# Delta twice in memory, slots per engine for the preparation of a unit, and the gate one step earlier

## The reference, cut to what matters

```python
xz = einsum('blc,ec->ble', xs, in_w); xi, z = xz[..., :d_inner], xz[..., d_inner:]
xi = silu(conv4(xi) + conv_b)
dt, Bm, Cm = split(einsum('bld,ed->ble', xi, xp_w))          # 6, 16 and 16 columns
delta = softplus(einsum('blr,dr->bld', dt, dt_w) + dt_b)
dA = exp(delta[..., None] * A)
dBu = delta[..., None] * Bm[:, :, None, :] * xi[..., None]
def step(h, inp):
    dA_t, dBu_t, C_t = inp
    h = dA_t * h + dBu_t
    return (h, einsum('bds,bs->bd', h, C_t))
y = (ys + xi * Dp) * silu(z)
out = einsum('bld,cd->blc', y, out_w)
```

## Time and profile before

| | us |
|---|---|
| median of 3 executions (5672.62 to 5676.45) | 5675.06 |
| the profiled execution | 5685.29 |
| its span, first to last instruction | 5683.5 |
| DVE busy | 3950.0 (69%) |
| PE busy | 3607.9 (63%) |
| ACT busy | 2759.5 (49%) |
| POOL busy | 2643.2 (47%) |

### The profile page before, as it was taken

The page is one execution under the profiler, slowest core; times in us unless marked ns, Lnnn a source line. Parts: engine busy times, 40 slices in busy tenths (PEclk is TensorE's granted clock), DMA queues, the critical chain, the costliest instruction groups (busy, mean ns, idle before and its releaser), DMA issues.

```text
span 5683.5 us, 44812 instructions
## 1 busy us (share of the span) xinstructions
PE 3607.9 (63%) x11400; PEld 1333.7 (23%) x11400; DVE 3950.0 (69%) x3478; ACT 2759.5 (49%) x3178; POOL 2643.2 (47%) x1276
## 2 busy tenths in 40 slices
PE   6566675666756667566675666656667566675666
PEld 2211222112321123211232112321123211232112
DVE  6478675786757867578675776748766487665876
ACT  4454454444544445444454544554545545455444
POOL 2266432664336643366433664336643365433664
PEclk8677786777767778677776777767777777776777
DMA  1367303663036630466304663046630466304762
GB/s 30 85 162 175 90 12 91 163 167 90 12 97 162 162 91 11 104 157 163 90 10 109 157 164 86 8 109 161 159 87 7 109 168 159 83 4 111 172 160 68
DMA packets 186995, 597.66 MB, mean 105 GB/s; under 512 B 30956, under 2 KB 31704, under 8 KB 185912
## 3 DMA queue, kind: packets, MB, share of 16 engines
q1 hardware_dynamic: 186680, 594.18, 42.5%
HBM read 485.03 MB, written 46.14 MB: 93 GB/s over the span
## 4 chain that ended last, share of the span: by engine, by line
issue 31%; PE 23%; DVE 21%; POOL 11%; ACT 9%; DMA 4%; SPq 1%; DVEq 0%; POOLq 0%; ACTq 0%
DVE ps L1152 7%; POOL arena L1242 5%; DVE arena L1157 4%; PE ps L620 4%; PE ps L612 4%; DVE arena L1045 3%; DMA arena<-dl 3%; POOL arena L1225 3%; PE ps L516 3%; POOL arena L1231 2%; PE ps L464 2%; PE ps L562 2%; PE ps L507 2%; PE ps L640 1%; ACT arena L746 1%
## 5 line engine op out<-in xcount | busy, mean ns | idle before, releaser
L1242 POOL TENSOR_TENSOR arena<-arena 128x1024 f32<-128x1024 f32 x768 | 1799.8, 2350 | 1268.1 <-DVE arena L1157 872.7
L1157 DVE TENSOR_TENSOR_SCAN arena<-arena,ps 128x1024 f32<-128x1024 f32 x768 | 1756.3, 2287 | 151.2 <-POOL arena L1242 38.1
L640 PE MATMUL ps<-arena,spread 96*128 96x512 bf16 x1536 | 611.5, 499 | 1115.5 <-DVE arena L1157 964.2
L880 ACT ACTIVATE arena<-arena,a_all 128x1024 f32<-128x1024 f32 x768 | 872.8, 1143 | 782.1 <-DMA arena<-dl 624.8
L1152 DVE TENSOR_TENSOR ps<-ps,arena 128x1024 f32<-128x1024 f32 x768 | 929.9, 1211 | 420.9 <-PE ps L640 420.9
L658 PE MATMUL ps<-arena,gather 128*32 128x512 f32 x3072 | 725.6, 846 | 83.1 <-POOL arena L1242 83.1
L1186 POOL TENSOR_TENSOR x<-x,arena 96x512 f32<-96x512 f32 x128 | 209.4, 1636 | 848.7 <-DVE arena L963 848.7
L640 PEld LDWEIGHTS ps<-arena,spread 96*128 96x128 bf16 x1536 | 120.7, 109 | 1778.4 <-DVE arena L1157 1328.1
L612 PE MATMUL ps<-arena,w_in 96*96 96x512 f32 x512 | 367.3, 885 | 63.2 <-DMA arena<-xq 63.2
L620 PE MATMUL ps<-arena,w_in 96*96 96x512 f32 x256 | 223.6, 1022 | 252.6 <-ACT arena L843 252.6
L1134 DVE TENSOR_TENSOR arena<-ps,arena 96x1024 f32<-96x1024 f32 x64 | 78.1, 1220 | 370.2 <-ACT arena L864 370.2
(11 more groups left out here) (149 smaller groups left out, 5409.6 us busy)
## 6 DMA issues: line engine op xcount, KB each, us to landing
arena<-dl SPq DMA_DIRECT2D x768, 512.0 KB, 5.4
arena<-bc SPq DMA_DIRECT2D x128, 512.0 KB, 6.2
arena<-arena SPq DMA_DIRECT2D x576, 64.0 KB, 2.2
dl<-arena SPq DMA_DIRECT2D x64, 384.0 KB, 3.5
xq<-in_x SPq DMA_DIRECT2D x8, 1536.0 KB, 8.9
arena<-xq SPq DMA_DIRECT2D x64, 192.0 KB, 3.8
out<-x SPq DMA_DIRECT2D x64, 192.0 KB, 2.1
arena<-xq SPq DMA_DIRECT2D x64, 191.8 KB, 3.2
```

The lines of the kernel that those rows point to most:

```text
L640: mm = pe.matmul(ps[:, bank + c, :], spread[:, r, :], sp[:, i, b, c * 512:(c + 1) * 512], start=True, stop=True)
L880: act.activation(da[:, m % DAS, :], dbc[:, m % DBC, :], ACT.Exp, scale=a_all[:, v // 2, m:m + 1]).then_inc(da_ready, 1)
L1157: dve.tensor_tensor_scan(hs[:, m % 2, :], da[:, m % DAS, :], driven, 0.0, ALU.mult, ALU.add).then_inc(h_ready, 1)
L1242: pool.tensor_tensor(pr[:, m % PRS, :], hs[:, m % 2, :], cmat[:, v % 2, :], ALU.mult).then_inc(pr_ready, 1)
```

## The change

Three things are changed together.

1. Layout: the partition of a state is now d * 16 + s. Delta is stored twice (`COPIES = 2`), as rows (channel, copy), so that one broadcast reads 16 different rows and writes each to 8 partitions in a row. `bmat` and `cmat` now take 16 rows one after the other, 8 times. `delta_out` counts 32 per unit.
2. Slots: each engine has its own. PE's z goes from slot 1 to slot 2, DVE's Delta from 4 to 5, ACT's first two parts from 5 and 6 to 7 and 8. On SP the xs copy goes to slot 5, the store of B and C to 6, the load of `bmat` to 7, the stores of Delta to 8, the load of `cmat` to 10, the parts to 10, 11 and 11.
3. Gate: S_GATE is 1. The silu of xi waits for the first sum of the unit before last (`y_acc`) and only the silu of z waits for its gate (`yz_ready`).

```diff
-S_XI, S_SILU, S_DT, S_SOFT, S_U, S_R, S_P2 = 0, 1, 3, 4, 5, 6, 7
-S_GATE, S_SKIP, S_OUT = 2, 4, 8
+PE_XI, PE_Z, PE_DT = 0, 2, 3
+ACT_SILU, ACT_DT, ACT_SOFT, ACT_P0, ACT_P1 = 1, 3, 4, 7, 8
+DVE_DELTA = 5
+POOL_U, POOL_R, POOL_P2 = 5, 6, 7
+SP_SHIFT, SP_BC, SP_B, SP_DL, SP_C = 5, 6, 7, 8, 10
+SP_P0, SP_P1, SP_P2 = 10, 11, 11
+S_GATE, S_SKIP, S_OUT = 1, 4, 8
...
                     sync.dma_start(dbc[:, m % DBC, :],
-                                   a["dl"][v % 2][g * DG:(g + 1) * DG, :].rearrange("(o d) n -> o d n", o=1)
-                                   .broadcast_to([NS, DG, L])).then_inc(dbc_in[m % DBC], 16)
+                                   a["dl"][v % 2][g * DG:(g + 1) * DG].rearrange("d c (o n) -> (d c) o n", o=1)
+                                   .broadcast_to([DG * COPIES, NS // COPIES, L])).then_inc(dbc_in[m % DBC], 16)
...
+                    if slot == SP_DL:
+                        sync.wait_ge(delta_ready, V + 1)
+                        for c in range(COPIES):
+                            sync.dma_start(a["dl"][i][:, c, :], delta).then_inc(delta_out, 16)
...
-                    if slot == S_SILU:
+                    if slot == ACT_SILU:
                         act.preload_act_table(ACT.Silu)
                         if v >= 2:
-                            act.wait_ge(yz_ready, V - 1)
+                            act.wait_ge(y_acc, (V - 2) * GPB + 1)
                         for c in range(2):
                             act.wait_ge(xi_ps, 2 * V + c + 1)
                             act.activation(xi[:, i, c * 512:(c + 1) * 512], ps[0:DI, 6 + c, :], ACT.Silu,
                                            bias=small_all[:, q, KC:KC + 1]).then_inc(xi_ready, 1)
+                        if v >= 2:
+                            act.wait_ge(yz_ready, V - 1)
                         for c in range(2):
                             act.wait_ge(z_ps, 2 * V + c + 1)
...
-    state_row = np.arange(128) % DG
+    state_row = np.arange(128) // NS
```

More of the change, by code:

```diff
@@ L52 @@
 DBC = 3
+COPIES = 2
 DAS = 3
@@ L391, in prep @@
                     q, i = divmod(v, 2)
-                    if slot == S_DT + 1:
+                    if slot == SP_SHIFT and v + 1 < UNITS and v >= 1:
+                        shifted(v + 1)
+                    if slot == SP_BC:
                         sync.wait_ge(bc_evac, V + 1)
                         sync.dma_start(a["bc"][i], bc_rows).then_inc(bc_out, 16)
[L395 to L399, removed]
+                    if slot == SP_B:
                         sync.wait_ge(bc_out, (V + 1) * 16)
@@ L402, in prep @@
                         if v >= 2:
-                            sync.wait_ge(pr_ready, (V - 1) * G)
[L404 to L408, removed]
+                            sync.wait_ge(bu_ready, (V - 1) * G)
+                        sync.dma_start(bmat[:, i, :], a["bc"][i][0:NS, :].rearrange("(o s) n -> o s n", o=1)
+                                       .broadcast_to([DG, NS, L])).then_inc(b_in, 16)
+                    if slot == SP_DL:
+                        sync.wait_ge(delta_ready, V + 1)
+                        for c in range(COPIES):
+                            sync.dma_start(a["dl"][i][:, c, :], delta).then_inc(delta_out, 16)
+                    if slot == SP_C:
+                        if v >= 2:
+                            sync.wait_ge(pr_ready, (V - 1) * G)
+                        sync.dma_start(cmat[:, i, :], a["bc"][i][NS:2 * NS, :].rearrange("(o s) n -> o s n", o=1)
+                                       .broadcast_to([DG, NS, L])).then_inc(c_in, 16)
+                    for k, at, done in ((0, SP_P0, part0), (1, SP_P1, part1), (2, SP_P2, part2)):
                         if slot == at:
@@ L601, in prep @@
                     q, i = divmod(v, 2)
-                    if slot == S_XI:
+                    if slot == PE_XI:
                         pe.wait_ge(xs_in[i], (p * QUADS + q + 1) * XSL)
@@ L615, in prep @@
                             mm.then_inc(xi_ps, 1)
-                    if slot == S_SILU:
+                    if slot == PE_Z:
                         for c in range(2):
@@ L622, in prep @@
                                       start=True, stop=True).then_inc(z_ps, 1)
-                    if slot == S_DT:
+                    if slot == PE_DT:
                         pe.wait_ge(sz_ready, 2 * V + 2)
@@ L849, in prep @@
                         exp_table()
-                    if slot == S_DT:
+                    if slot == ACT_DT:
                         bias = small_all[:, q, KC + 1:KC + 2]
@@ L859, in prep @@
                         act.activation(two(6, DI), two(6, DI), ACT.Relu, bias=bias).then_inc(soft_act, 1)
-                    if slot == S_SOFT:
+                    if slot == ACT_SOFT:
                         act.wait_ge(soft_act, V * 4 + 1)
@@ L864, in prep @@
                         act.activation(soft, soft, ACT.Ln, bias=eps[0:DI, 2:3]).then_inc(soft_act, 1)
-                    if slot == S_U:
+                    if slot == ACT_P0:
                         act.wait_ge(u_ready, V + 1)
@@ L869, in prep @@
                         act.activation(parts[0], u, ACT.Copy).then_inc(part0, 1)
-                    if slot == S_R:
+                    if slot == ACT_P1:
                         act.wait_ge(rest1, V + 1)
```

18 lines of the change are left out of this document (9 added, 9 removed).

## The result

| | before | after |
|---|---|---|
| median, us | 5674.52 | 5981.31 |
| lowest to highest | 5672.62 to 5676.45 | 5974.86 to 6002.02 |
| span of the profiled execution | 5683.5 | 5979.4 |

The ratio is 1.0547, with an interval of 1.0521 to 1.0573: 5.5% slower, where I had forecast 5% faster.

What follows compares the result with a forecast made beforehand. DVE's scan stage, stalled behind PE and ACT, was the bound. 492 us go and 91, 73 and 25 come: 303, taken as 295; 5685 - 295 = 5390 profiled, 5380 median. Own range 5330 to 5430, 8-in-10 range 5270 to 5580.

Steps and rivals of the forecast that it cites:

- The row-per-engine read: Delta's broadcasts reading one row per engine: no gain in rate taken, from windows at 231 against 235 GB/s.
- the 1.3 us at each unit border: New DVE wait at 7 unit borders per pair for late parts of u, 0 to 3 us, taken as 1.3; 73 in all.
- Transfers: SP's queue after Delta's stores: SP stands until 13, last part issued near 20 and landed at about 25.5 us.
- Gate and xi: DVE's early gate waits for the sum after xi on PE, 1.1 to 2.8 us, taken as 1.9; 91 in all.
- z one slot later: PE runs z after u for step 3, so DVE's 5.46 us wait goes, covered by ACT's lead of two steps.
- the 5.46 us: DVE's gap in the followed unit, waiting for u for step 3 queued behind z on PE; forecast to go.
- Delta one slot later: DVE asks for Delta after the sixth scan, so its 2.41 us wait for ACT goes, with little to spare.
- Later parts: ACT's copies and POOL's splitting after Delta: DVE's 0.62 us scan wait for POOL in the unit counted as gone.
- parts in time: Rival: the parts of u arrive in time at unit borders, 73 us more gained, 5307; chance 0.18.
- Slower: Rival: repeated row reads queue behind each other in Delta's broadcast; 0.5 us a packet gives 5975; chance 0.06.
- The parts arrive much later: Rival: parts 3 to 4 us late at unit borders instead of 1.3, 140 us more, 5520; chance 0.11.
- TensorE stays at its low level: Rival: PE's z, dt, skip product and first sum double, scans behind POOL slip about 4 us, 5572; chance 0.14.

## Why the prediction was wrong

Two steps failed. The first is "The row-per-engine read ... I take no gain". I took the old pattern of `bmat` and `cmat` as a stand-in for the new pattern of Delta, found it no slower than Delta's old one, 231 against 235 GB/s, and stopped. The loads didn't run alone in that window, so the reading was looser than I said; its conclusion held, since Delta's new pattern costs some 6 us, within the spread. But the same edit turned `bmat` and `cmat` the other way, to 8 copies in front, and I never gave that pattern a price. The change says it in words, and the Trainium skill's page "DMA: Bandwidth & Descriptors", which I cited for its bandwidth, has the rule. The runs put 323 us in its place, with 8 packets at once where there had been 16. I even wrote that `bmat` "hid already"; it did as a wait, but as a load it stands in the queue ahead of Delta's store.

The second is the 1.3 us at each unit border, in "Transfers". With `bmat` and `cmat` mended the multiply waits 426.7 us in all:

```profile
PE ps L651 <- DMA arena<-arena: 537.9, 64, 18.9
...
DVE ps L1165 <- PE ps L651: 426.7, 95, 13.4
...
DVE arena L1155 <- PE ps L669: 110.9, 64, 6.2
...
DVE arena L1170 <- POOL arena L1255: 63.9, 82, 1.0
```

Less 107 for the pair starts that is 320, or 5.7 a border and not 1.3 (in the changed kernel itself, with 760.1, it is 11.7); 56 x 4.4 = 246 of the 278 us by which that kernel's 5658 is above 5380. Two more terms nearly close the sum. The scan's wait for POOL, which I had counted as gone, is 64 us. The gate's wait, which I had priced at 91, is 110.9 less 8 x 6.2 for the last gates of the pairs, 62 us, so 29 less: 246 + 64 - 29 = 281.

The chain was the one I had described, and longer at each link. From the sixth scan's start (1119.05 in the changed kernel; 1065.44 in the one with the two loads on all engines, in a unit whose border wait is 6.7 us), by SP's and PE's rows:

| | forecast | `bmat`, `cmat` on all engines | changed kernel |
|---|---|---|---|
| SP free again | 13 | 14.7 | 16.6 |
| last part issued | 20 | 22.9 | 25.8 |
| PE released | 25.5 | 30.5 | 35.1 |

I had let the queue move 2.7 MB at 0.24 MB a us. With the two loads on all engines 3.3 MB went by from the end of SP's wait to PE's release, at 211 GB/s with a share of 0.96. In the changed kernel it was 187 GB/s from 1135.7 to 1154.1, and `bmat` alone moved at 139.

By differences, from the kernel with early slots and the old layout up to the changed one: 5368 + 204 (late slots) + 81 (second store) + 6 (Delta's pattern) + 323 (`bmat` and `cmat` on half the engines) = 5982. These add up because each is the difference of two neighbours; in another order they would be shared out otherwise, as the 92 us instead of 323 for the same two loads in the kernel before show.

The other steps.

- "Gate and xi": the new wait of 1.1 to 2.8 us, taken as 1.9, came as 1.95 in the unit shown, but as little as 0.94 in others. Over the whole trace it is 113.0 - 49 = 64 us, not 91; once the parts were in time (5367.90) it was 165.9 - 49 = 117. Undoing it there gave 93, so the agreement with 91 is luck. What I missed is that nothing asked for it: I took over the change's trade, and the better half of it could be had alone.
- "z one slot later": z is behind u and the 5.46 us are gone. I put that down to both edits together. Each undone alone costs 213 us for the wait for the gate and 19 for the slot. The 213 has the clock in it: before, z took 3.73 us in the unit of the earlier trace rows, now 1.88.
- "Delta one slot later": right, 2.41 us gone, only 16 waits left, two in each pair: the one before its first scan (28.6 us in the first pair) and one in its first unit (2.1).
- "Later parts": the scan's wait for POOL, counted as gone, rose from 38.1 to 63.6 us.
- The forecast 5380 lies near the 5368 of the kernel with early slots and the old layout, but that is luck: for parts in time I had 5307. The gate's wait, 117 us for 91, is 26 of the 61 us between; the rest I can't place.

The rivals. The forecast for "Slower" was 5975, next to the measured 5981, by a wrong mechanism: a price of 0.5 us a packet for the repeats of a row. The packets weren't slow; half of the engines had none. "The parts arrive much later" named the right place, with 3.8 us instead of 12. "TensorE stays at its low level" had little part: z took 1.88 us at a granted clock of 1.00. The low level did come to dt and the skip product in some units (3.23 and 3.51 us in one, against 1.88), but DVE's scans waited for POOL, through which I had let it act, only some 25 us more than before, not 192.

## What to carry to other kernels

When a layout changes, write down for each transfer that touches it, not for the one that the change is about, which dimension stands outermost in the source pattern and how long it is; then look for a window in which that transfer really runs alone and read the DMA share; here 0.52 went with 8 packets at once instead of 16. No row shows a wait for the slow loads themselves; their price came up at the store and the parts behind them in the queue, the store being one that SP must see landed. And test the parts of a bundled change one by one: here the wait for the sum was worth 213 us and z's slot 19, while the early gate cost 93, the late slots 204 (in the old layout), and the layout with its second store 410.

## What the runs showed of the hardware

- A load whose source pattern has 8 outermost (8 copies of 16 rows, or 8 rows 16 times each) held the 16 transfer engines at a share of 0.51 to 0.52, had 8 to 10 packets under way at once, and moved 125 to 139 GB/s; the same bytes with 16 rows outermost had 16 to 18 under way for 1.45 of 2 us and moved 231 GB/s at 0.87.
- Writing each of 16 rows to 8 partitions in a row, or 8 rows 16 times over, made no difference for Delta (5658 and 5653 us).
- 128 slow loads of 512 KB cost 92 us in the kernel before and 323 in the changed one, whose slots and second store both differ.
- TensorE, after waiting 3.27 us, ran z in 3.63 us at a granted clock of 0.53; after waiting 0.85 us it ran it in 1.96 at 1.00.
- One more store of 384 KB a unit cost 81 us over 64 units, 1.3 each, near the 1.6 us that its bytes take at 235 GB/s.
